# Vector engine's side work moved between the score slots of two softmax attentions

## The reference

```python
# stage 2, causal: 16 heads of 8 features, rotary q and k, every row sees all rows before it in its sequence
x = x + _L0_attn_ref(_layernorm(x, axis=-1), L0_attn_w_qkv, L0_attn_w_out)
# stage 11, blocked: the same, but a row sees only rows of its own block of 32
att = jnp.einsum('bhnqd,bhnkd->bhnqk', qb, kb) * scale
att = jnp.where(causal, att, jnp.finfo(att.dtype).min)
att = jax.nn.softmax(att, axis=-1)
out = jnp.einsum('bhnqk,bhnkd->bhnqd', att, vb)
```

## Time and profile before

| | |
|---|---|
| time of the runs, median (lowest to highest of 3) | 3836.42 us (3836.40 to 3842.51) |
| the profiled execution's own time | 3806.29 us |
| its span in the trace | 3804.9 us |
| causal attention in the trace | about 174 to 578 us |
| blocked attention in the trace | about 3393.5 to 3722 us |
| busy share of the whole span | PE 81%, DVE 62%, ACT 46%, POOL 18% |

### The profile page before, as it was taken

One profiled execution on the slowest core, in us unless ns is written; L12 is line 12 of the kernel. 1 busy time (PEld: TensorE's weight loads), 2 busy tenths in 40 slices (PEclk: granted clock), 3 DMA queues, 4 the chain that ended last, 5 costly groups with the idle time before them and its releaser, 6 DMA issues. The chain is left out here.

```text
span 3804.9 us, 77157 instructions
## 1 busy us (share of the span) xinstructions
PE 3076.8 (81%) x29994; PEld 2350.2 (62%) x29994; DVE 2371.4 (62%) x8684; ACT 1763.2 (46%) x3303; POOL 666.9 (18%) x1005
## 2 busy tenths in 40 slices
PE   4788887648588466888889999999997799858883
PEld 2366664336366354555578888888887566536673
DVE  5756648863356743555577777777777555574447
ACT  1133431124234233444378988888986444313320
POOL 0000001150542421111022222222222000010001
PEclk9789987779778678999999999999999899956765
DMA  5000000014100033000000000000000000000000
GB/s 166 1 2 3 3 3 1 6 34 136 59 20 5 25 91 111 12 12 12 1 1 11 11 1 11 11 11 1 11 1 1 1 1 1 1 0 3 3 3 23
DMA packets 77611, 76.90 MB, mean 20 GB/s; under 512 B 8249, under 2 KB 65986, under 8 KB 77122
## 3 DMA queue, kind: packets, MB, share of 16 engines
q1 hardware_dynamic: 69058, 55.17, 4.8%
q0 software_dynamic: 8192, 16.79, 1.5%
HBM read 45.07 MB, written 26.87 MB: 19 GB/s over the span
## 5 line engine op out<-in xcount | busy, mean ns | idle before, releaser
L136 POOL TENSOR_SCALAR rstd<-mean_var 128x4 f32<-128x4 f32 x96 | 27.9, 291 | 1907.4 <-DVE mean_var L127 1907.4
L2141 ACT ACTIVATE shared_floats<-bank,L_b 128x512 f32<-128x512 f32 x208 | 142.9, 687 | 374.0 <-PE bank L1980 368.1
L2066 DVE SCALAR_TENSOR_TENSOR shared_floats<-bank,L_b,shared_floats 128x512 f32<-128x512 f32 x208 | 155.6, 748 | 254.8 <-ACT shared_floats L2141 245.7
L2003 PEld LDWEIGHTS bank<-ffn,shared_floats 128*128 128x128 f32 x1664 | 220.2, 196 | 151.4 <-DVE shared_floats L2075 95.1
L1611 PE MATMUL bank<-shared_floats 32*128 32x32 f32 (+4 forms) x2048 | 225.2, 348 | 78.0 <-DVE shared_floats L1756 48.5
L165 PE MATMUL bank<-ident,xn 128*128 128x128 f32 x320 | 65.7, 342 | 262.1 <-DVE xn L153 203.1
L2284 PE MATMUL bank<-layer,shared_floats 128*128 128x128 f32 x2048 | 273.5, 277 | 0.0
L2003 PE MATMUL bank<-ffn,shared_floats 128*128 128x128 f32 x1664 | 229.6, 282 | 45.7 <-DVE shared_floats L2075 45.7
L1611 PEld LDWEIGHTS bank<-shared_floats 32*128 32x128 f32 x2048 | 176.4, 220 | 125.4 <-DVE shared_floats L1756 64.6
L1756 DVE TENSOR_REDUCE shared_floats<-bank 128x2 f32<-128x256 f32 (+3 forms) x320 | 134.6, 470 | 189.9 <-PE bank L1625 189.4
L2576 ACT ACTIVATE shared_floats<-bank,layer 128x256 f32<-128x256 f32 x512 | 209.4, 471 | 93.7 <-PE bank L2271 93.7
(11 more groups left out here) (299 smaller groups left out, 8312.7 us busy)
## 6 DMA issues: line engine op xcount, KB each, us to landing
shared_floats<-bins SPq DMA_DIRECT2D x32, 320.0 KB, 4.2
results<-shared_floats SPq DMA_DIRECT2D x32, 320.0 KB, 3.5
expert_weights<-in_dram_experts SPq DMA_DIRECT2D x32, 312.0 KB, 3.1
layer<-in_dram_layers SPq DMA_DIRECT2D x8, 902.0 KB, 4.5
bins<-zero SPq DMA_DIRECT2D x1, 5760.0 KB, 22.6
ffn<-in_ffn SPq DMA_DIRECT2D x1, 2496.0 KB
bins<-xn,f_bin_row POOLq DMA_INDIRECT x128
results<-results,result_rows POOLq DMA_INDIRECT x128
```

The lines of the kernel that those rows point to most:

```text
L2003: m = T.matmul(k.bank[7][:, tile(t)], hid[:, tile(t)], down_w[:, tile(r)], start=False, stop=(r == ROWS2 - 1), skip_group_check=True)
L2066: V.scalar_tensor_tensor(out=act[:, :], in0=k.bank[3 + g % 2 * 2][:, :], scalar=b13[:, 2 * r + 1:2 * r + 2], in1=act[:, :], op0=ALU.add, o ...
L2141: A.activation(act[:, :], k.bank[2 + g % 2 * 2][:, :], ACT.Identity, bias=b13[:, 2 * r:2 * r + 1]).then_inc(k.sem("f2_identity"), 1)
```

## The change

In the causal order, VectorE's parts of batch n-1 move from the end of batch n-1 to behind maxima 0 of batch n; stats move from ahead of maxima 0 to behind maxima 1; apply from behind divide to behind maxima 2; heads 1 from ahead of maxima 4 to behind it; add from ahead of maxima 5 to behind it. Since parts of n-1 now run after maxima 0 of n, `at_tops` becomes two tiles. In the blocked order, project 0 and heads 0 move from slot 1 to slot 0 (behind maxima 0, ahead of weigh and divide), project 1 and heads 1 take their place in slot 1, stats move behind divide, out now stands behind project 1 and heads 1, apply ahead of add, and parts stay behind add.

```diff
--- before.py
+++ after.py
@@ -1747,7 +1747,7 @@
 
     def maxima(n, p):
         n, rd, rows, g = a.pair(n, p, False)
-        rd, tops = a.rounds_a[rd], k.sb("at_tops", [P, 4 * BLOCKS])
+        rd, tops = a.rounds_a[rd], k.sb(f"at_tops{n % 2}", [P, 4 * BLOCKS])
         V.wait_ge(k.sem("at_scored_a"), a.u0 // 2 + g + 1)
         for r in rows:
             bank, at = k.bank[4 + r % 2], 0
@@ -1760,7 +1760,7 @@
 
     def parts(n):
 
-        tops, parts = k.sb("at_tops", [P, 4 * BLOCKS]), k.sb("at_parts", [P, BLOCKS * P], BF16)
+        tops, parts = k.sb(f"at_tops{n % 2}", [P, 4 * BLOCKS]), k.sb("at_parts", [P, BLOCKS * P], BF16)
         high, rest = k.sb("at_high", [P, 4 * BLOCKS], BF16), k.sb("at_rest", [P, 4 * BLOCKS])
         V.wait_ge(k.sem("at_max"), a.u0 + (n + 1) * a.units)
         if n:
@@ -1895,19 +1895,21 @@
 CAUSAL_A = [[(b, 0, 256) for b in (6, 7)], [(b, 0, 192) for b in (4, 5)],
             [(b, 0, 128) for b in (2, 3)] + [(b, 0, 64) for b in (0, 1)]]
 CAUSAL_B = [[(b, b * BK, S) for b in blocks] for blocks in ((0, 1), (2, 3, 4), (5, 6, 7))]
-CAUSAL_ORDER = [("stats", 0, 0), ("score", 0, 0), ("values", 0, 0), ("copy values", 0, 0),
-                ("score", 1, 0), ("weigh", 1, 2), ("shifts", 0, 1), ("copy shifts", 0, 1), ("project", 0, 0), ("heads", 0, 0),
-                ("score", 2, 0), ("values", 1, 0), ("copy values", 1, 0),
-                ("score", 3, 0), ("weigh", 2, 2), ("divide", 0, 2), ("project", 1, 0), ("heads", 1, 0), ("apply", 0, 0),
-                ("score", 4, 0), ("out", 0, 2), ("add", 0, 2), ("values", 2, 0), ("copy values", 2, 0), ("turn", 0, 0),
+CAUSAL_ORDER = [("score", 0, 0), ("parts", 0, 1), ("values", 0, 0), ("copy values", 0, 0),
+                ("score", 1, 0), ("stats", 0, 0), ("weigh", 1, 2), ("shifts", 0, 1), ("copy shifts", 0, 1), ("project", 0, 0),
+                ("heads", 0, 0),
+                ("score", 2, 0), ("apply", 0, 0), ("values", 1, 0), ("copy values", 1, 0),
+                ("score", 3, 0), ("weigh", 2, 2), ("divide", 0, 2), ("project", 1, 0),
+                ("score", 4, 0), ("heads", 1, 0), ("out", 0, 2), ("values", 2, 0), ("copy values", 2, 0), ("turn", 0, 0),
                 ("copy turned", 0, 0), ("q heads", 0, 0), ("k heads", 0, 0),
-                ("score", 5, 0), ("weigh", 0, 1), ("values", 3, 0), ("copy values", 3, 0), ("parts", 0, 0)]
+                ("score", 5, 0), ("add", 0, 2), ("weigh", 0, 1), ("values", 3, 0), ("copy values", 3, 0)]
 BLOCKED_A = [[(b, b * BK, b * BK + BK) for b in range(BLOCKS)]]
-BLOCKED_ORDER = [("stats", 0, 0), ("score", 0, 0), ("weigh", 0, 3), ("divide", 0, 3), ("values", 0, 0), ("copy values", 0, 0),
-                 ("score", 1, 0), ("shifts", 0, 1), ("copy shifts", 0, 1), ("project", 0, 0), ("heads", 0, 0),
-                 ("values", 1, 0), ("copy values", 1, 0), ("out", 0, 3), ("add", 0, 3), ("project", 1, 0), ("heads", 1, 0),
-                 ("apply", 0, 0), ("values", 2, 0), ("copy values", 2, 0), ("turn", 0, 0), ("copy turned", 0, 0),
-                 ("q heads", 0, 0), ("k heads", 0, 0), ("values", 3, 0), ("copy values", 3, 0), ("parts", 0, 0)]
+BLOCKED_ORDER = [("score", 0, 0), ("project", 0, 0), ("heads", 0, 0), ("weigh", 0, 3), ("divide", 0, 3), ("stats", 0, 0),
+                 ("values", 0, 0), ("copy values", 0, 0),
+                 ("score", 1, 0), ("shifts", 0, 1), ("copy shifts", 0, 1), ("project", 1, 0), ("heads", 1, 0),
+                 ("values", 1, 0), ("copy values", 1, 0), ("out", 0, 3), ("apply", 0, 0), ("add", 0, 3), ("parts", 0, 0),
+                 ("values", 2, 0), ("copy values", 2, 0), ("turn", 0, 0), ("copy turned", 0, 0),
+                 ("q heads", 0, 0), ("k heads", 0, 0), ("values", 3, 0), ("copy values", 3, 0)]
 BLOCKED_B = BLOCKED_A
 CAUSAL = Softmax("L0_wqkvT", CAUSAL_A, CAUSAL_B, 8, 2, CAUSAL_ORDER)
 BLOCKED = Softmax("L3_wqkvT", BLOCKED_A, BLOCKED_B, 4, 3, BLOCKED_ORDER, CAUSAL)
```

## The result

The changed kernel takes 3787.51 us (median of 3 runs, 3785.62 to 3790.79), the kernel before 3836.42. The ratio is 0.987, 95% interval 0.985 to 0.989: 49 us, 1.3% faster. On another chip, with more runs, it is 3787.31 against 3825.32 (23 runs), ratio 0.989 (0.985 to 0.992), 38 us. The forecast was 3823, 13.6 us faster, and its range ended at 3808. The direction is right, the size is not.

A forecast was written before the change was run, and what follows sets the result against it. TensorE sets the time, lengthened by its waits for VectorE's maxima and rotary sums. Terms -9.7 - 3.8 + 2.2 - 2.3 = -13.6 us, from the median 3836.4, give 3823 us; range 3808 to 3833.

The forecast's parts named there:

- Part 1: Causal, even batches: parts and stats out of the way of maxima 0 shrink the gap before slot 1; 9.7 us gained.
- the margin ahead of slot 2: Causal, even batches: maxima 1, now behind parts, still come 0.4 us before TensorE wants them.
- Part 3: Causal, odd batches: heads 1 behind maxima 4 let slot 5 and the next slot 0 start earlier; 3.8 us gained.
- Part 5: Clock: fewer half-rate stretches in causal even slots 1, half of 4.5 us taken, 2.3 gained; blocked clock taken as 0.
- Part 4: Blocked, odd batches: project 0 and heads 0 into slot 0, heads 0 still waiting for slot 1; +2.2 us in sum.
- 9.2 against 8.5: Blocked, odd batches from the third chunk: chain after against before at full clock, a loss of 0.7 us each.
- both ends: Blocked clock: weigh and slot 1 may speed up (up to 12 us), or project 1 run at half (3.6 lost).
- Rival C: Blocked: mean clock falls from 0.69 to 0.64, total +10 us, 3846; decides from 0.66 down; chance 0.07.
- The base: Sum made against the profiled execution's 3806.3 us; the 30 us up to the runs' median carried over unchanged.
- -15.9 + 8.1: Whole kernel: no clock gain and project 1 at half give -7.7 us, the limit of what measurement can tell.

The follow-up runs named there:

- run 12: Kernel before with only heads 1 of the causal stage moved behind maxima 4: 3824.08 us, ratio 1.000.
- run 3: New causal order with two tiles for the maxima, old blocked order, against the kernel before: 3805.11 us, ratio 0.994.
- run 6: Kernel before with only project 0 of the blocked stage moved to slot 0, heads 0 left behind slot 1: 3816.13 us, ratio 0.997.
- after again: The changed kernel measured again with no edit, beside the kernel before on one chip: 3787.31 us, ratio 0.989.
- run 4: New blocked order, old causal order with the two tiles for the maxima kept, against the kernel before: 3799.13 us, ratio 0.992.
- run 5: Kernel before with only project 0 and heads 0 of the blocked stage moved to slot 0, project 1 still behind out: 3827.05 us, ratio 1.001.
- run 8: Changed kernel with a third q buffer, so heads 0 need not wait for slot 1: 3777.52 us, ratio 0.987 to the kernel before.
- run 10: Changed kernel with three q buffers, blocked project 1 and heads 1 in slot 0, causal heads 0 behind maxima 2: 3763.48 us, ratio 0.984 to before.

## Why the prediction was right about the waits and wrong about the size

**Part 1 (parts and stats), right:** -9.7 predicted, -8.9 measured alone; the gap 0.41, the margin ahead of slot 2 intact. One of the seven gaps it counts was 0.42 in the execution read and could not shrink; in three other executions of the old order it was 1.2 to 1.3. **Part 3 (heads 1), right in its place:** the gap is 0.68 where 0.5 was predicted, and "parts gone from behind maxima 5 leave VectorE free there" turned out to be a condition: without part 1 the gain is nil (run 12). **Part 5, the causal clock, too small:** 2.3 us taken. The causal means fell by 19.3, of it 11.6 idle time and 7.7 busy time for the same matmuls. 4.6 of the 7.7 lie in the even slots 1 (from their first matmul to that of slot 2: 30.2 us of busy time in the mean of the old order, 25.6 in every execution with the new one), where the forecast looked for them: its full 4.5 came, and the half was the mistake. The other 3.1 are spread over other slots, and no run ties them to a move. Windows of the kernel after over two even slots 1 (behind gaps of 0.41 us), and between them the slots 1 and 3 of an odd batch, whose gaps of 1.42 and 1.81 the change left:

```profile
276.90:279.90 3.00, 3.00 (x86) 2.48 (x87) 2.86 (x18) 0.78 (x3) 0.00 (x0) 1.00 0.03 8
340.20:343.20 3.00, 2.98 (x60) 2.09 (x64) 2.86 (x18) 0.55 (x2) 0.00 (x0) 0.66 0.03 8
350.10:353.10 3.00, 2.96 (x77) 2.66 (x77) 1.02 (x2) 1.03 (x2) 0.00 (x0) 0.72 0.03 5
409.30:412.30 3.00, 3.00 (x86) 2.48 (x86) 2.86 (x18) 0.80 (x3) 0.00 (x0) 1.00 0.02 5
```

Over the same 3 us, all seven even slots 1 with the short gap were granted 1.00 in the kernel after, in its repeat and in run 3; three of six were at 0.50 for a while behind 1.96. The Trainium skill, "TensorE: Matmul & The Clock Gate", section "What's actually happening", makes half rate the idle default that activity releases. For the gap of 0.41 this trace agrees: the clock stays at 1.00. Behind 1.42 and 1.81 us it fell in ten of 13 slots all the same. The forecast had 4.5 us as the full value and halved it. It had one execution to take it from, and that one had the least busy time in this stage of the five with the old order (332.2 us, mean 339.8; the new order has a mean of 332.1).

**Part 4 (blocked), wrong, and the largest miss:** +2.2 us predicted, 18.3 gained. The order of events was right down to VectorE's stand behind `at_scored_b`. The step that failed is the sentence that prices it: "Take the end of slot 1 as 0, full clock", from which "9.2 against 8.5" came. The rows quoted in the same text had project 0 at 3.76 us, at a granted clock of 0.50. I put 2.0 for it, and left the clock of the rest as it was ("I take 0 and keep both ends"). Both ends came. Project 0 runs at full rate ahead of weigh in most batches and lifts what follows it (run 6 shows this with project 0 moved alone), and project 1 takes 3.5 us in the mean. Windows of 7.2 us from maxima 0 on, three odd batches of the kernel before:

```profile
3463.72:3470.92 7.20, 6.14 (x249) 5.93 (x249) 3.12 (x5) 0.78 (x3) 0.00 (x0) 0.59 0.02 5
3498.19:3505.39 7.20, 4.68 (x240) 4.39 (x240) 2.93 (x4) 0.79 (x3) 0.00 (x0) 0.80 0.02 5
3533.45:3540.65 7.20, 5.79 (x232) 5.59 (x234) 2.94 (x4) 0.66 (x2) 0.00 (x0) 0.50 0.02 5
```

and the same three of the kernel after:

```profile
3461.82:3469.02 7.20, 6.18 (x245) 4.79 (x246) 0.76 (x2) 0.69 (x3) 0.00 (x0) 0.91 0.02 5
3493.98:3501.18 7.20, 6.00 (x252) 4.51 (x252) 0.95 (x3) 0.97 (x4) 0.00 (x0) 1.00 0.01 2
3527.39:3534.59 7.20, 6.04 (x252) 4.61 (x252) 0.84 (x3) 0.85 (x4) 0.00 (x0) 1.00 0.02 5
```

The clock is the last column but two: 0.59, 0.80 and 0.50 became 0.91, 1.00 and 1.00. Over all six odd batches that have the wait the mean goes from 0.70 to 0.93. In the other four executions with the old blocked order it is 0.75 to 0.83, in the other two with the new one 0.90 and 0.92, so the lift is some 0.14 in the mean and the first pair shows it too large. The terms of the sum, as means over these six batches (five executions with the old order; three with the new one, from after, after again and run 4):

| | forecast | measured |
|---|---|---|
| what project 0 adds to the stretch from maxima 0 to the end of slot 1 | +2.0 | +0.2 (7.2 to 7.4) |
| end of slot 1 to the next slot 0, before | 8.5 | 10.1 |
| the same, after | 7.2 | 7.9 |
| next slot 0 to its maxima | no change | -0.3 (3.7 to 3.4) |
| a batch | +0.7 | -2.3 |

So the chain before was longer than priced by project 0 at half rate. The chain after is longer by less, since heads 1 wait for divide and maxima 1 anyway: with project 1 at 3.78 us they start 0.96 us after those. And the clock lift pays for project 0 in its new place. That is 14 us in six batches. The first three batches, with chunk 1, where heads 0 do not wait, gave 5.3 (means of 51.9 and 46.5 us; single executions 49.7 to 55.1 and 45.4 to 48.1) where 2.0 was predicted. Together 19.4; the rest of the stage gave 1.1 back.

**Rival C, out by its own measure:** it decided from a mean clock of 0.66 down, and the stage has 0.71 (0.69 in the kernel after run again).

**The base, wrong:** "I carry the difference over unchanged". The sum was made against an execution at 3806.3, and its 30 us to the median were taken as a constant. The later comparisons put the kernel before between the two, at medians of 3824.9 to 3827.8: the 3806.3 was a lucky execution, and the first median (3 runs, on another chip) lay high, by chance or by the chip. The miss of 35 us (3822.8 to 3787.5) is thus some 20 us of the blocked stage, 3.5 of the causal one, and 11 of that first median. That the profiled execution of after came out at 3790.8, next to the 3792.7 worked out for it, is luck: the missing gain and the lucky execution cancelled. In the forecast, "-15.9 + 8.1" should read -15.8; the -7.7 stands.

## What to carry to other kernels

Price a moved group of matmuls at the rate that its own rows show, in the old place and in the new one: here four 128x512 matmuls took up to 3.8 us right behind slots of 32-column work, and 2.0 in most batches where they stood ahead of them. Before a wait is moved ahead on an in-order engine, look for what stands behind it and give TensorE something independent to do in that time (run 5 gained nothing, the whole change 18 us); then ask which buffer makes the wait (run 8, another 13.5 us of the stage). And when one execution of the profile is 30 us away from the median, work out stage lengths as bands, not as numbers.

## What the runs showed of the hardware

**Half clock at a busy TensorE.** In the kernel after, slot 0 behind an odd batch, and the project 1 ahead of it:

```profile
3503.10:3506.80 3.70, 3.70 (x5) 1.63 (x6) 2.77 (x4) 2.49 (x4) 0.00 (x0) 0.50 0.02 4
3509.00:3512.90 3.90, 3.90 (x108) 3.90 (x110) 2.31 (x17) 0.00 (x0) 0.00 (x0) 0.50 0.02 4
```

Both stretches are busy throughout and both were granted 0.50, that is 1.2 GHz; idle times of 1.93 and 1.25 us stand ahead of them. The 32-column slot stays at half although it never pauses. In the causal stage of the kernel after, from chunk 1 on, no slot behind a gap of 0.2 to 1.22 us had a lowered clock, and of the 13 slots behind gaps of 1.42 and 1.81 ten had (windows of 3 us from the start of each). Yet in run 10 two of eight slots 3 of the odd batches had a lowered clock behind a gap of 1.22, though TensorE was at 1.00 ahead of it. One of them:

```profile
385.71:388.71 3.00, 3.00 (x77) 2.74 (x78) 2.79 (x6) 1.03 (x2) 0.00 (x0) 0.74 0.00 0
```

What decides whether a half-rate stretch follows a gap is open.

**A stage's time scatters by its clock.** With the old order, five executions of the causal stage had 402.9 to 415.2 us at idle times of 68.9 to 71.8; the 12 us between them are busy time (332.2 to 345.4 us), so the same matmuls at another rate. With the new order six executions have 389.4 to 392.5: the stage became faster and also steadier.
